# Gate-weight loads of a two-layer kernel issued by GpSimd instead of SyncE

## The chip, the cores and the metric

The program runs on one core of one Trainium2 chip. The metric is the device time of one execution in microseconds (us), median of three runs. The engines are named as the profile names them: PE (TensorE), DVE (VectorE), ACT (ScalarE), POOL (GpSimd) and SP (SyncE, which only issues transfers here). SPq is SP's sequencer.

## The reference, cut to what matters

Two layers on x of shape (8, 256, 128), float32. Each layer is x + s * silu(f), where s is a causal attention and f a mixture of experts, both of the layer-normed x. The change touches the experts of the second layer:

```python
logits = xn @ Wr + br                       # (T, 32)
aff = sigmoid(logits)
top_v, top_i = top_k(aff, 8)
w_full[t, top_i] = top_v / (sum(top_v) + 1e-9)     # gate weight per token and expert
gate = silu(einsum('th,ehi->eti', xn, Wg) + bg)    # 32 experts, 64 inner columns each
up = einsum('th,ehi->eti', xn, Wu) + bu
down = einsum('eti,eih->eth', gate * up, Wd) + bd
routed = einsum('te,eth->th', w_full, down)
```

The kernel multiplies the gate branch of each expert by its token weights before the down projection, so the sum over experts becomes one accumulation on PE.

## The kernel before

The 2048 tokens are cut into 4 chunks of 512. Inner columns stand on the 128 partitions and tokens run along the free axis, so two experts (2 x 64 columns) fill one tile. A chunk has 16 such pairs and a 17th step for the shared expert: step n of `gate`, `up` and `down` is pair n % 17 of chunk n // 17.

The order of all work is one list written out by hand, `PROGRAM` (lines 87 to 141). Every engine walks the same list and does its own part of each step, in that order, waiting on semaphores for the other engines. An engine never goes past a step whose semaphore has not come. The steps that matter here:

- `weights1/c`: PE turns the gate weights of chunk c, ACT copies them, SP stores them in a scratch tensor in HBM (L553).
- `wb/n`: the weights of two pairs are read back from that scratch, each row spread over 64 partitions by a broadcast read. There are two loads, 64 x 2 x 512 float32 each, into slot n % 2 of the two slots of `wb`. The step waits for the store and for `s_ga_done` at 2 (n - 1), which says that the multiplications that read the slot last are done. There are 32 such steps, 64 loads. Before the change they stand on SP at L554 to L563.
- `gate/n`: PE multiplies (L754), ACT makes tanh into `gt` (L1002) and the linear part into `gb` (L1005), POOL multiplies `gb` by the spread weights in `wb` (L1098). It waits for ACT and for both loads of the slot, and counts up `s_ga_done`.
- `up/n`: PE multiplies (L763) after the result of the expert before it is ready, since there is one PSUM bank. DVE makes `h` from `gt` and `gb` (L1274), then from the bank (L1281).
- `down/n`: PE adds `h` times wd to the accumulator (L775).
- `max` and `score`: attention scores in units. DVE takes maxima (L1302), or ACT takes the exponential (L1020) and POOL cuts it to the causal part in place (L1091), in `pk`, which `values` on PE reads (L850).
- `norm/c/b`: POOL raises a 128x32 tile to the power -0.5 (`orms`, L1102); `norm0` and `norm1` do so with a 128x4 tile (L1064, L1075).
- `fetch/c/b`: SP issues 24 loads of split queries and keys into `qa` and `ka` (L540); `store/c` issues the 12 stores before them (L524), `minus/c/b` two small copies (L548).

SP issues everything in this kernel before the change: weights, inputs, stores, fetches and the `wb` loads, all on one queue. POOL issues no transfer. The slots give a `wb` step a place well ahead of its use: `wb/1`, say, comes two list entries after `gate/1`, and the first multiplication that reads it is in `gate/2`. The program reserves 1024 bytes of each partition for descriptors of transfers that POOL issues.

Of the kernel before, what the change touches and what calls it, by code (L numbers as in the profile page):

```python
# [45 lines left out]
E1, INNER = 32, 64  # L46
# [98 lines left out]
def build(nc, t):  # L145

    with ExitStack() as ctx:
# [359 lines left out]
        def _(sp):  # L507
            def steps(program):
                for step in program:
                    kind, c, *rest = step  # L510
                    if kind == "load":
                        if c >= 2:
                            sp.wait_ge(s_var1, at(2 * (c - 2), "var1", 1))
                        sp.dma_start(x_of[side(c)], t["x"][c]).then_inc(s_x_in[c % 2], 16)
                    elif kind == "store":

                        for n in range(2):
                            for a in range(3):
                                done, name = ((s_part1, "part1"), (s_part2, "part2"), (s_part3, "part3"))[a]
                                for f in range(2):  # L520
                                    r = a if n == 0 else 2 - a
                                    sp.wait_ge(done, at(c, name, 2 * n + f + 1))
                                    dst = t["parts_dram"][c, n, f * 2 * GH:(f + 1) * 2 * GH, :, r * DH:(r + 1) * DH, :]
                                    sp.dma_start(dst, parts[:, a, 2 * n + f, :]).then_inc(s_parts_stored[f], 16)  # L524
                    elif kind == "fetch":
                        b = rest[0]
                        for f in range(2):
                            heads = slice(f * 2 * GH, (f + 1) * 2 * GH)
                            sp.wait_ge(s_parts_stored[f], at(c, "parts_stored", 16 * 6))
                            if c:  # L530
                                sp.wait_ge(s_sc_ps, unit(c - 1, b, 2 * f + 1, 2) + 1)
                            else:
                                sp.wait_ge(s_rooms, 3)
                            for n, dst in enumerate((qa, ka)):
                                for m in range(2):
                                    row = m * HALF
                                    for width in (3, 2, 1):
                                        first = 0 if n == 0 else 3 - width
                                        src = t["parts_dram"][c, n, heads, m, first * DH:(first + width) * DH, b * SEQ:(b + 1) * SEQ]
                                        sp.dma_start(dst[row:row + width * DH, b, heads, :],  # L540
                                                     src.rearrange("h r t -> r h t")).then_inc(s_qk_in[b][f], 16)
                                        row += width * DH
                    elif kind == "minus":
                        b = rest[0]
                        sp.wait_ge(s_mrow_sb, at(c, "mrow_sb", b + 1))
                        for m in range(2):
                            row = m * HALF + TERMS
                            sp.dma_start(qa[row:row + 3, b, :, :],  # L548
                                         mrows[m * 3 * HEADS:(m + 1) * 3 * HEADS, b * SEQ:(b + 1) * SEQ]).then_inc(s_mrow_in, 16)
                    elif kind == "weights1":  # L550

                        sp.wait_ge(s_wt_sb, at(c, "wt_sb", 1))
                        sp.dma_start(t["wt_dram"][c], hs[INNER:INNER + E1, c % 2, :]).then_inc(s_wt_stored, 16)  # L553
                    elif kind == "wb":  # L554

                        k, slot = c % (PAIRS // 2), c % 2
                        sp.wait_ge(s_wt_stored, at(c // (PAIRS // 2), "wt_stored", 16))
                        if c >= 2:
                            sp.wait_ge(s_ga_done, 2 * (c - 1))
                        src = t["wt_dram"][c // (PAIRS // 2)].rearrange("(j e) t -> e j t", e=2)  # L560
                        for e in range(2):
                            sp.dma_start(wb[e * INNER:(e + 1) * INNER, slot, :, :],
                                         src[e, 2 * k:2 * k + 2, :].partition_broadcast(INNER)).then_inc(s_wb_in[slot], 16)  # L563
                    elif kind == "fin":
                        sp.wait_ge(s_out_done, at(c, "out_done", 1))
                        sp.dma_start(t["out"][c], out[:, :, :]).then_inc(s_out_stored, 16)
# [473 lines left out]
        def _(pool):  # L1040
# [19 lines left out]
            for step in PROGRAM:  # L1060
# [25 lines left out]
                elif kind == "score":  # L1086
# [3 lines left out]
                    pool.wait_ge(s_pk_done, unit(c, b, g, u) + 1)  # L1090
                    pool.affine_select(out=dst, in_=dst, compare_op=ALU.is_ge, fill=0.0, base=0,  # L1091
                                       pattern=[[0, heads], [1, P]], channel_multiplier=-1).then_inc(s_pk_masked, 1)
                elif kind == "gate" and c % STEPS < PAIRS:
                    j = c % STEPS
                    k = (c // STEPS * PAIRS + j) // 2
# [323 lines left out]
```

## Time and profile before

| what | value |
|---|---|
| median of 3 runs | 533.67 us |
| the runs | 528.33, 536.59, 533.67 us |
| profiled execution, its own time | 529.14 us |
| its span | 527.1 us |
| PE, DVE, ACT, POOL busy | 482.0, 398.0, 286.7, 264.5 us |
| mean granted clock of PE | 0.984 |

The span runs from the first to the last instruction of the profiled execution. Busy time counts an engine's instructions and leaves out waits, branches and the issue of transfers. The three runs lie 1.5% apart. A window is given in microseconds from the start of the span.

### The profile page before, as it was taken

What the parts mean: (1) busy time and instruction counts of PE and PEld (TensorE: products, weight loads), DVE (VectorE), ACT (ScalarE), POOL (GpSimd) and SP (SyncE); (2) the same over time, 40 slices, a digit from 0 to 9 for tenths busy, and PEclk for the clock granted to TensorE, in tenths of its full rate; (3) what the DMA queues carried; (4) which work ended last, traced back from release to release, by engine and by line L of the source; (5) the groups of instructions that cost most, each with busy time, mean ns of one, the idle gap of its engine ahead of it and who ended that gap; (6) DMA issues with size and microseconds to landing.
All of it is one profiled execution on the core that took longest, in us unless ns stands there. A gap on an engine that the chain in (4) does not pass through costs nothing.

```text
span 527.1 us, 8723 instructions
## 1 busy us (share of the span) xinstructions
PE 482.0 (91%) x3104; PEld 234.7 (45%) x3104; DVE 398.0 (76%) x796; ACT 286.7 (54%) x456; POOL 264.5 (50%) x223
## 2 busy tenths in 40 slices
PE   3898798589998999999999999999999999999995
PEld 3645444233543444544344554454344444444442
DVE  2326387788987888677999888569988988977674
ACT  1342563215775644557775654546775556567741
POOL 6040153104634447735767622716754749456962
PEclk9999799889999999999999999999999999999999
DMA  7800149851069553012369083101563561131201
GB/s 281 295 1 0 44 116 156 131 100 45 1 164 141 100 87 81 5 60 62 103 137 158 14 136 65 44 21 42 159 117 90 86 124 42 40 85 40 74 8 41
DMA packets 49627, 46.04 MB, mean 87 GB/s; under 512 B 6352, under 2 KB 39216, under 8 KB 48944
## 3 DMA queue, kind: packets, MB, share of 16 engines
q1 hardware_dynamic: 49584, 45.48, 38.6%
q8 instruction: 25, 0.41, 0.3%
q14 instruction: 18, 0.15, 0.1%
HBM read 37.47 MB, written 7.60 MB: 86 GB/s over the span
## 4 chain that ended last, share of the span: by engine, by line
PE 63%; DVE 16%; issue 6%; POOL 5%; DMA 4%; SPq 3%; ACT 3%; DVEq 0%; POOLq 0%; ACTq 0%
PE bank L763 8%; PE bank L775 8%; PE bank L754 7%; PE scores L795 6%; PE bank L850 4%; PE scores L789 4%; DVE nmax L1302 3%; DVE h L1274 3%; SPq L540 2%; POOL gb L1098 2%; PE scores L690 2%; PE scores L681 2%; PE scores L728 2%; PE scores L684 2%; DMA wb<-wt_scratch 2%
## 5 line engine op out<-in xcount | busy, mean ns | idle before, releaser
L1098 POOL TENSOR_TENSOR gb<-gb,wb 128x512 f32<-128x512 f32 x64 | 83.4, 1303 | 119.7 <-ACT gb L1005 111.4
L1302 DVE TENSOR_REDUCE nmax<-scores 128x4 f32<-128x1024 f32 (+1 forms) x96 | 114.3, 1217 | 20.0 <-PE scores L795 19.6
L1020 ACT ACTIVATE pk<-scores 128x1024 f32<-128x1024 f32 x96 | 95.8, 1023 | 28.2 <-PE scores L795 27.9
L1091 POOL TENSOR_SCALAR_AFFINE_SELECT pk<-pk 128x512 f32<-128x512 f32 (+1 forms) x96 | 82.2, 861 | 45.2 <-ACT pk L1020 44.6
L1002 ACT ACTIVATE gt<-bank,bgh 128x512 f32<-128x512 f32 (+1 forms) x68 | 46.8, 688 | 61.6 <-PE bank L754 49.0
L763 PE MATMUL bank<-xnt,wu 128*128 128x512 f32 x128 | 68.3, 616 | 1.1 <-DVE h L1281 1.1
L754 PE MATMUL bank<-xnt,wg 128*128 128x512 f32 x128 | 68.2, 615 | 0.9 <-ACT gb L1005 0.9
L775 PE MATMUL bank<-h,wd 128*128 128x512 f32 x128 | 68.5, 625 | 0.1
L1274 DVE SCALAR_TENSOR_TENSOR h<-gt,gb 128x512 f32<-128x512 f32 x64 | 56.7, 885 | 10.9 <-POOL gb L1098 10.6
L1281 DVE SCALAR_TENSOR_TENSOR h<-bank,bu,h 128x512 f32<-128x512 f32 x64 | 48.1, 751 | 16.2 <-PE bank L763 14.5
L789 PE MATMUL scores<-mask_h,ident_h 64*128 64x256 bf16 (+2 forms) x384 | 38.4, 279 | 10.1 <-DVE nmax L1302 8.4
L1102 POOL TENSOR_TENSOR orms<-oms,minus_half 128x32 f32<-128x32 f32 x8 | 44.7, 5591 | 0.4 <-DVE oms L1335 0.3
L1005 ACT ACTIVATE gb<-bank,bg 128x512 f32<-128x512 f32 x64 | 43.7, 683 | 0.0
L795 PE MATMUL scores<-ka,qa 48*128 48x256 bf16 (+1 forms) x512 | 38.0, 247 | 0.0
L850 PE MATMUL bank<-pk,v 128*32 128x512 f32 x256 | 34.1, 605 | 1.8 <-DVE o L1322 1.6
L795 PE MATMUL scores<-qa,ka 51*128 51x128 bf16 (+1 forms) x512 | 34.0, 245 | 0.6 <-DVE nmax L1302 0.6
L789 PEld LDWEIGHTS scores<-mask_h,ident_h 64*128 64x128 bf16 x384 | 12.9, 95 | 47.1 <-issue 21.4
L795 PEld LDWEIGHTS scores<-qa,ka 51*128 51x128 bf16 x512 | 16.7, 94 | 36.5 <-issue 16.4
L775 PEld LDWEIGHTS bank<-h,wd 128*128 128x128 f32 x128 | 21.6, 191 | 19.7 <-issue 16.4
L1027 ACT ACTIVATE ot<-bank 128x512 f32<-128x512 f32 x32 | 19.2, 599 | 20.4 <-PE bank L855 20.2
L763 PEld LDWEIGHTS bank<-xnt,wu 128*128 128x128 f32 x128 | 21.2, 189 | 19.7 <-issue 13.4
L1085 POOL TENSOR_TENSOR parts<-qkf,parts 128x512 bf16<-128x512 f32 x16 | 18.9, 1204 | 20.6 <-ACT parts L967 20.6
(247 smaller groups left out, 728.3 us busy)
## 6 DMA issues: line engine op xcount, KB each, us to landing
wb<-wt_scratch SPq DMA_DIRECT2D x64, 256.0 KB, 4.2
parts_scratch<-parts SPq DMA_DIRECT2D x48, 128.0 KB, 2.4
qa<-parts_scratch SPq DMA_DIRECT2D x32, 96.0 KB
ka<-parts_scratch SPq DMA_DIRECT2D x32, 96.0 KB
qa<-parts_scratch SPq DMA_DIRECT2D x32, 64.0 KB
ka<-parts_scratch SPq DMA_DIRECT2D x32, 64.0 KB
ha<-in_wkq SPq DMA_DIRECT2D x1, 1024.0 KB, 4.9
wb<-in_wvo SPq DMA_DIRECT2D x1, 1024.0 KB, 7.4
```

The source lines that it names most:

```text
L754: m = mm(bank[5], wg[:, j * P:(j + 1) * P], xnt1[:, c % 2, :], start=True, stop=True)
L763: mm(bank[6], wu[:, j * P:(j + 1) * P], xnt1[:, c % 2, :], start=True, stop=True).then_inc(s_up_ps, 1)
L775: m = mm(bank[7], wd[:, j, :], h1[:, n % HR, :], start=(j == 0), stop=False)
L789: mm(s[m][:, :, cols - P + part * HALF:cols], ident_h[half, 1 - m + part, :], late.unsqueeze(1).to_broadcast([HALF, per, P - part * HALF]) ...
L795: last = mm(s[m][:, h, :], stat[half, b, h0 + h, row:row + P], move[half, b, h0 + h, tile0:tile0 + width], start=(h == 0 and not masked), ...
L850: mm(o[32 * hh:32 * hh + 32, :, :], v1[:, 2 * b, head, :], pk0[g % 2][:, 2 * hh:2 * hh + 2, :], start=True, stop=False, skip_group_check=True)
L1020: A(dst.rearrange("p (h m) q -> p m h q", m=2), pairs[pair_of(step)][:, :, :].rearrange("p m (h q) -> p m h q", q=cols), ACT.Exp, scale=SC ...
L1091: pool.affine_select(out=dst, in_=dst, compare_op=ALU.is_ge, fill=0.0, base=0, pattern=[[0, heads], [1, P]], channel_multiplier=-1).then_i ...
L1098: pw(gb[:, c % 2, :], gb[:, c % 2, :], wb[:, k % 2, j % 2, :], ALU.mult).then_inc(s_ga_done, 1)
L1274: link(V.scalar_tensor_tensor(out=h, in0=gt[0:rows, n % 2, :], scalar=1.0, in1=gb[0:rows, n % 2, :], op0=ALU.add, op1=ALU.mult))
L1281: V.scalar_tensor_tensor(out=h, in0=up, scalar=bu[0:rows, j:j + 1], in1=h, op0=ALU.add, op1=ALU.mult).then_inc(s_h_done, 1)
L1302: V.tensor_reduce(dst, src, AX, ALU.max, negate=True).then_inc(s_nmax_done, 1)
```

## The change

The branch for `wb` leaves the program of SP and stands in that of POOL, with the same two waits, the same two transfers and the same semaphores. The list is the same, so POOL now issues each pair of loads when it comes to that place among its own multiplications, masks and powers.

```diff
@@ SP @@
-                    elif kind == "wb":
-
-                        k, slot = c % (PAIRS // 2), c % 2
-                        sp.wait_ge(s_wt_stored, at(c // (PAIRS // 2), "wt_stored", 16))
-                        if c >= 2:
-                            sp.wait_ge(s_ga_done, 2 * (c - 1))
-                        src = t["wt_dram"][c // (PAIRS // 2)].rearrange("(j e) t -> e j t", e=2)
-                        for e in range(2):
-                            sp.dma_start(wb[e * INNER:(e + 1) * INNER, slot, :, :],
-                                         src[e, 2 * k:2 * k + 2, :].partition_broadcast(INNER)).then_inc(s_wb_in[slot], 16)
@@ POOL, between the branches for score and gate @@
+                elif kind == "wb":
+
+                    k, slot = c % (PAIRS // 2), c % 2
+                    pool.wait_ge(s_wt_stored, at(c // (PAIRS // 2), "wt_stored", 16))
+                    if c >= 2:
+                        pool.wait_ge(s_ga_done, 2 * (c - 1))
+                    src = t["wt_dram"][c // (PAIRS // 2)].rearrange("(j e) t -> e j t", e=2)
+                    for e in range(2):
+                        nc.gpsimd.dma_start(wb[e * INNER:(e + 1) * INNER, slot, :, :],
+                                     src[e, 2 * k:2 * k + 2, :].partition_broadcast(INNER)).then_inc(s_wb_in[slot], 16)
```

The next rows are the order of instructions on POOL around `wb/0` and `wb/1`, at the first experts of the first chunk. A row has the line, the operation, the tiles and how many stand in a row. Before:

```order
L1064 TENSOR_TENSOR rstd<-vare,minus_half 128x4
L1098 TENSOR_TENSOR gb<-gb,wb 128x512
L1075 TENSOR_TENSOR rstd<-vare,minus_half 128x4
L1098 TENSOR_TENSOR gb<-gb,wb 128x512 x5
L1091 AFFINE_SELECT pk<-pk 128x4x128 x2
```

And with the change, where every line number of POOL is 10 smaller except that of `gate`:

```order
L1091 DMA wb<-wt_scratch 64x2x512 x2
L1054 TENSOR_TENSOR rstd<-vare,minus_half 128x4
L1098 TENSOR_TENSOR gb<-gb,wb 128x512
L1065 TENSOR_TENSOR rstd<-vare,minus_half 128x4
L1098 TENSOR_TENSOR gb<-gb,wb 128x512
L1091 DMA wb<-wt_scratch 64x2x512 x2
L1098 TENSOR_TENSOR gb<-gb,wb 128x512 x2
```

The loads of `wb/0` now come before the power of `norm0/2`, and those of `wb/1` between the multiplications of `gate/1` and `gate/2`.

The second place is POOL late in the last chunk, from `gate/60` to `gate/63`. Before:

```order
L1098 TENSOR_TENSOR gb<-gb,wb 128x512
L1091 AFFINE_SELECT pk<-pk 128x4x128
L1091 AFFINE_SELECT pk<-pk 128x1024
L1102 TENSOR_TENSOR orms<-oms,minus_half 128x32
L1098 TENSOR_TENSOR gb<-gb,wb 128x512
L1091 AFFINE_SELECT pk<-pk 128x4x128 x2
L1098 TENSOR_TENSOR gb<-gb,wb 128x512
L1091 AFFINE_SELECT pk<-pk 128x1024
L1091 AFFINE_SELECT pk<-pk 128x4x128
L1098 TENSOR_TENSOR gb<-gb,wb 128x512
```

With the change:

```order
L1091 DMA wb<-wt_scratch 64x2x512 x2
L1098 TENSOR_TENSOR gb<-gb,wb 128x512
L1081 AFFINE_SELECT pk<-pk 128x4x128
L1081 AFFINE_SELECT pk<-pk 128x1024
L1102 TENSOR_TENSOR orms<-oms,minus_half 128x32
L1091 DMA wb<-wt_scratch 64x2x512 x2
L1098 TENSOR_TENSOR gb<-gb,wb 128x512
L1081 AFFINE_SELECT pk<-pk 128x4x128 x2
L1098 TENSOR_TENSOR gb<-gb,wb 128x512
L1091 DMA wb<-wt_scratch 64x2x512 x2
L1081 AFFINE_SELECT pk<-pk 128x1024
L1081 AFFINE_SELECT pk<-pk 128x4x128
```

The loads of `wb/29`, `wb/30` and `wb/31` stand ahead of `gate/60`, ahead of `gate/61` and behind `gate/62`.

## Rows read from the trace of the kernel before

**Rows 1.** The page: busy time of each engine, then the chain that ended last.

```profile
PE 482.0 (91%) x3104; PEld 234.7 (45%) x3104; DVE 398.0 (76%) x796; ACT 286.7 (54%) x456; POOL 264.5 (50%) x223
...
PE 63%; DVE 16%; issue 6%; POOL 5%; DMA 4%; SPq 3%; ACT 3%; DVEq 0%; POOLq 0%; ACTq 0%
```

**Rows 2.** Stretches: window, length, busy PE, PEld, DVE, ACT, POOL, clock, DMA, GB/s.

```profile
77.00:105.00 28.00, 20.05 (x118) 10.61 (x118) 20.07 (x48) 9.82 (x19) 9.24 (x8) 0.92 0.87 140
...
485.00:502.00 17.00, 16.60 (x99) 6.98 (x98) 11.47 (x18) 13.53 (x19) 17.00 (x13) 1.00 0.26 63
```

**Rows 3.** Waits: who waited for whom, total us, times, longest us.

```profile
SPq L559 <- POOL gb L1098: 130.5, 16, 20.3
...
PE scores L789 <- DMA ka<-parts_scratch: 1.4, 1, 1.4
```

**Rows 4.** The tile wb: duration ns min/median/max, first and last start; landing.

```profile
L562 SPq DMA_DIRECT2D wb<-wt_scratch x64: 573/607/643, 77.0 to 498.5; - x64
L1098 POOL TENSOR_TENSOR gb<-gb,wb x64: 1257/1270/1774, 82.3 to 510.2; 128x512 f32<-128x512 f32 x64
...
DMA to landing us min/median/max: 3.6/4.2/9.6
```

**Rows 5.** Timeline of POOL, 76 to 101: start, us, what, [idle before <- releaser].

```profile
76.74 2.50 POOL L1081 TENSOR_TENSOR pk<-pk 128x512 f32<-128x512 f32 x2 [2.22 <-ACT pk L937]
...
82.26 1.26 POOL L1098 TENSOR_TENSOR gb<-gb,wb 128x512 f32<-128x512 f32 x1 [1.60 <-DMA wb<-wt_scratch]
...
90.87 1.26 POOL L1098 TENSOR_TENSOR gb<-gb,wb 128x512 f32<-128x512 f32 x1
98.51 2.48 POOL L1098 TENSOR_TENSOR gb<-gb,wb 128x512 f32<-128x512 f32 x2 [6.37 <-DMA wb<-wt_scratch]
```

**Rows 6.** Timeline of DVE and PE, 99 to 104.

```profile
99.87 1.66 DVE L1274 SCALAR_TENSOR_TENSOR h<-gt,gb 128x512 f32<-128x512 f32 x1 [3.08 <-POOL gb L1098]
...
103.51 0.50 PE L789 MATMUL scores<-mask_h,ident_h 64*128 64x256 bf16 x4 [5.33 <-DVE nmax L1302]
```

**Rows 7.** Timeline of POOL, 436 to 448.

```profile
436.48 1.68 POOL L1091 TENSOR_SCALAR_AFFINE_SELECT pk<-pk 128x1024 f32<-128x1024 f32 x2
...
439.72 5.83 POOL L1102 TENSOR_TENSOR orms<-oms,minus_half 128x32 f32<-128x32 f32 x1 [0.29 <-DVE oms L1335]
...
446.56 1.27 POOL L1098 TENSOR_TENSOR gb<-gb,wb 128x512 f32<-128x512 f32 x1
```

**Rows 8.** Timeline of DVE and PE behind that, at experts 51 and 52.

```profile
450.60 0.75 DVE L1281 SCALAR_TENSOR_TENSOR h<-bank,bu,h 128x512 f32<-128x512 f32 x1 [0.54 <-PE bank L763]
...
452.25 1.02 PE L763 MATMUL bank<-xnt,wu 128*128 128x512 f32 x2
```

**Rows 9.** Timeline of POOL, DVE and PE around `wb/27` and `gate/57`.

```profile
468.21 1.09 POOL L1091 TENSOR_SCALAR_AFFINE_SELECT pk<-pk 128x1024 f32<-128x1024 f32 x1 [0.85 <-ACT pk L1020]
...
474.28 0.68 DVE L1274 SCALAR_TENSOR_TENSOR h<-gt,gb 128x512 f32<-128x512 f32 x1
...
479.30 1.12 PE L763 MATMUL bank<-xnt,wu 128*128 128x512 f32 x2
```

**Rows 10.** Timeline of POOL and DVE, 480 to 502.

```profile
480.99 2.19 POOL L1091 TENSOR_SCALAR_AFFINE_SELECT pk<-pk 128x1024 f32<-128x1024 f32 x2
484.92 1.27 POOL L1098 TENSOR_TENSOR gb<-gb,wb 128x512 f32<-128x512 f32 x1 [1.73 <-ACT gb L1005]
484.94 1.80 DVE L1274 SCALAR_TENSOR_TENSOR h<-gt,gb 128x512 f32<-128x512 f32 x1
...
493.63 1.27 POOL L1098 TENSOR_TENSOR gb<-gb,wb 128x512 f32<-128x512 f32 x1
...
501.21 1.04 DVE L1274 SCALAR_TENSOR_TENSOR h<-gt,gb 128x512 f32<-128x512 f32 x1 [0.43 <-POOL gb L1098]
```

**Rows 11.** DVE's L1274: the page's group, then its durations ns min/median/max.

```profile
L1274 DVE SCALAR_TENSOR_TENSOR h<-gt,gb 128x512 f32<-128x512 f32 x64 | 56.7, 885 | 10.9 <-POOL gb L1098 10.6
...
L1274 DVE SCALAR_TENSOR_TENSOR h<-gt,gb x64: 673/683/1797, 83.6 to 513.0; 128x512 f32<-128x512 f32 x64
```

## The prediction

> **What bounds the kernel now.** I read the page first. PE is busy 91% of the span and POOL half of it, and the chain that ended last runs 63% on PE, 16% on DVE and 5% on POOL [rows 1]. POOL has 262 us of idle time, so its added work costs only where another engine waits for it. The windows show where that may be. Near the start, from 77 to 105, PE is busy 20.05 of 28 us and the DMA engines 0.87 of the time. From 485 to 502 POOL is busy 17.00 of 17 us [rows 2]. Then the waits: SP stands 130.5 us before `wb` steps, waiting for POOL's multiplications to free a slot, while PE waits only 1.4 us for any transfer [rows 3]. So the time that SP gets back buys little. Last, the tile `wb`: SP takes 0.607 us to issue one load, POOL 1.27 us for one multiplication, and a load lands 4.2 us after its issue (3.6 to 9.6) [rows 4].
>
> **The change, part by part.** SP loses 64 issues of 0.607 us, 39 us, and its 130.5 us of waits [rows 3, 4]. Queued behind them on SP are the `fetch`, `store` and `minus` steps. They may come earlier, but PE waits 1.4 us in all for such a load [rows 3]. I count nothing for it and keep the 1.4 us for a rival.
>
> POOL gains 64 issues, two at each of 32 places. No row shows a transfer issued by POOL. The low bound is SP's 0.607 us, the high one 4.2 us, if POOL were held until the load has landed [rows 4]. I take 1.3 us, from the nearest row of POOL's own, the 1.27 us multiplication [rows 4]. A pair then costs 2.6 us and all of them 83 us, which would bring POOL to 348 us busy, 66%. The Trainium skill, page "DMA: Bandwidth & Descriptors", section "Latency and other measured facts", gives about 1 us to the first byte of a transfer issued by POOL and 0.6 us for one by SP; SP's row agrees, and an estimate of the sum with 1.0 us an issue is 8 us in place of the 12 below.
>
> The added wait for `s_ga_done` costs nothing by itself: at each place in the list POOL has already run the multiplications that it counts, as the places below show. What is new is that a load starts when POOL gets there, and that everything of POOL behind it starts later. The data is there 1.3 + 4.2 = 5.5 us after the place (the second load's issue starts 1.3 us in). Three places are priced.
>
> Start. POOL reaches `wb/0` at 76.74 + 2.50 = 79.24, so the data lands at 84.7 and `gate/0` starts 2.5 us later than its 82.26 [rows 5]. DVE waits for it, and what follows shifts. `gate/1` then ends at 92.13 + 2.5 = 94.6, which is the place of `wb/1`; its data comes at 100.1 with the median landing, 1.6 us after the 98.51 at which `gate/2` starts now, and at 105.5, 7.0 us after, with the longest landing of 9.6 us, which is that of this very load in a full queue [rows 4, 5]. DVE waits 3.08 us for this `gate/2` and PE 5.33 us for DVE [rows 6], so the lateness reaches PE. The two ends are 1.6 and 7.0; nothing places it nearer to one, since its own queue is new and the DMA engines are as full as before. I take the middle, 4.3 us.
>
> `wb/24` and `wb/25`. They stand between the two masks that start at 436.48 and ahead of the power at 439.72. One more mask stands there, at half of 1.68 us. So the power cannot start before 436.48 + 1.68 + 0.84 + 5.2 = 444.2, 4.5 us late. POOL then runs to `gate/51` without idle time, so that starts at 451.1 instead of 446.56 and ends at 452.3 [rows 7]. DVE's two operations of 0.68 and 0.75 us then end at 453.8, against 451.35 [rows 8, 11]; PE's next `up`, at 452.25, had 0.9 us to spare [rows 8]. On the path: 2.4 - 0.9 = 1.5 us.
>
> `wb/29` to `wb/31`. `wb/29` comes at 480.99 + 2.19 = 483.18, POOL is free at 485.8, and `gate/60` moves from 484.92 by 0.9 us. From there POOL has no idle time. `wb/30` stands before `gate/61` at 493.63 and `wb/31` before `gate/63`, 2.6 us each, and DVE waits for `gate/63` at 501.21 [rows 2, 10]. Nothing is left to take the lateness up: 0.9 + 2.6 + 2.6 = 6.1 us.
>
> Elsewhere it is hidden. `wb/27` is the closest case: place 469.30, data 474.8, `gate/57` done at 476.1, 1.8 us after DVE took it, and DVE's second operation ends near 477.6, before PE's next `up` at 479.30 [rows 9]. If that cover of 1.7 us were gone, the rest of 1.8 us would go on the path, as it would at two or three places like it.
>
> Sum: 4.3 + 1.5 + 6.1 = 11.9 us. The profiled execution took 529.14 us for a span of 527.1, so the changed one would take 541.0. It lies 4.5 us under the median of 533.67, and the changed kernel's runs will scatter in the same way, so I forecast 533.67 + 11.9 = **546 us** for the median. With 0.607 us an issue the same places give about 1 + 0 + 2.4 us, 537; with 2.6 us, twice my value, about 6 + 8 + 14 us, 562.
>
> **The rivals.** About 2%, 10.7 us, is what a measurement of this kernel can tell from no change; the bounds are 523.0 and 544.3.
>
> My forecast's mechanism with its own range, 538 to 551: 0.40. It straddles the bound, with half on each side.
>
> *Absorbed.* POOL is idle half of the time and an issue costs hardly more than on SP: 537. For it speaks that most `wb` places have 5 us or more to the first use; against it, that 485 to 502 has no idle time. 0.25. The Trainium skill says, on the same page, section "Issuing engines are not separate DMA queues", that a change of the issuing engine saves or costs only the sequencer's time, usually a small one; this would be that case.
>
> *DVE is held too.* One L1274 takes 1.80 us beside a POOL multiplication at 484.94 where its median is 0.683 [rows 10, 11]. All 64 take 56.7 us against 64 x 0.683 = 43.7, 13 us more, beside 264.5 us of POOL work. If an issue holds DVE as a multiplication does, 83 us of them add 13 x 83 / 264.5 = 4 us there, and as much in DVE's other operations: 546 + 8 = 554, if it all lies on the path; 0.12. The Trainium skill, page "SBUF — State Buffer", section "SBUF: two separate sides", has DVE and POOL share a port pair that one locks for a whole instruction, and warns that some DVE copies keep POOL from writing descriptors. The trace agrees for POOL's computing; no row shows an issue.
>
> *A dear issue.* At 2.6 us each, 562; 0.12. If POOL is held until each load has landed, 4.2 us, it has 269 us more work than now and would be the bound in order: the last three pairs alone cost 24 us, the whole over 590; 0.04.
>
> *Faster.* The loads get a queue of their own. Before, `wb/1` took 9.6 us behind the 24 fetch loads of SP and POOL stood idle 6.37 us for it [rows 4, 5]. If POOL's loads are served in turn with SP's and an issue is as cheap as on SP, `gate/2` comes earlier, at most by the 3.08 us that DVE waits; with PE's 1.4 us for `ka` that is 4.5 us [rows 3, 6], 529 us. It decides the sign only where an issue costs less than about 0.6 us, so that the late stretch costs nothing. The Trainium skill, page "DMA: Bandwidth & Descriptors", section "Queues, rings and completion order", says that a DMA engine takes its queues in turn, which speaks for it; no row has two queues at work. 0.07, of which 0.03 is over 2% faster.
>
> That the change does not do what it says is excluded: the order of POOL has all 64 loads.
>
> **How the numbers follow.** Faster by over 2%: 0.03. Slower by over 2%: half of the forecast's 0.40 and a little of its upper side, 0.22, and the three dear cases, 0.12 + 0.12 + 0.04, together 0.50. Within 2%: the rest, 0.47. The range, 8 times in 10, reaches from the cheap end, 533, to the twice as dear issue, 562; left out are most of the faster case, the longest case and half of the dear one.
>
> **What would show it.** Rows of POOL issuing `wb` near 1.3 us confirm the price; at 0.6 or 2.6 the sum fails there. The start term is right if `gate/2` starts 2 to 7 us later than 98.51; the late one if POOL has no idle time between `gate/60` and `gate/63` and that stretch is 5 to 7 us longer, with DVE's wait for L1098 above its 10.6 us. DVE is held too if L1274's mean rises above 885 ns. The forecast is wrong if POOL's sequencer waits long before the loads, if the loads land later than 4.2 us, or if PE's idle time does not grow while POOL's does.

## The result: 570.5 us, outside the range

The changed kernel took 570.49 us (median of 4 runs, 568.73 to 577.32) beside 533.77 us for the kernel before on the same chip: ratio 1.0695, 95% interval [1.0596, 1.0794]. Run again it took 569.8 us, ratio 1.0716 [1.0644, 1.0789]. The forecast was 546 us with a range of 533 to 562. The direction was right, and the size was wrong by a factor of three: 37 us in place of 12. The profile after is that of the repeated run, because the profiled execution of the first was a disturbed one. Its span is 568.6 us, 41.5 more than before; the traces show more than the 37 us of the medians, since the profiled execution of the kernel before lay 4.5 us under its median.

The page of the changed kernel, busy time and then the chain that ended last, the answer to [rows 1]:

```profile
PE 498.7 (88%) x3104; PEld 241.0 (42%) x3104; DVE 407.8 (72%) x796; ACT 287.3 (51%) x456; POOL 299.8 (53%) x287
...
PE 52%; POOL 13%; DVE 12%; issue 9%; DMA 8%; ACT 4%; SPq 1%; POOLq 0%; DVEq 0%; ACTq 0%
```

POOL is busy 35 us longer, but that is not the loss by itself: POOL is still idle for almost half of the span. PE has the same 3104 instructions and is busy 16.7 us longer, at a mean granted clock of 0.950 where it was 0.984. The other 24.8 us are idle time of PE.

Its tile `wb`, the answer to [rows 4]: duration ns min/median/max, first and last start, then the landing.

```profile
L1091 POOL DMA_DIRECT2D wb<-wt_scratch x64: 587/596/805, 82.0 to 537.9; - x64
L1098 POOL TENSOR_TENSOR gb<-gb,wb x64: 1250/1268/1776, 91.1 to 551.7; 128x512 f32<-128x512 f32 x64
...
DMA to landing us min/median/max: 3.5/4.2/9.6
```

An issue costs POOL 0.596 us, less than half of the 1.3 us that I took and no more than it cost SP. The median landing is as before. So neither number of the sum was worse than assumed, and the loss was still three times the sum.

Its waits, the answer to [rows 3]: who waited for whom, total us, times, longest us.

```profile
POOL gb L1098 <- DMA wb<-wt_scratch: 28.1, 5, 9.1
DVE h L1274 <- POOL gb L1098: 26.9, 8, 6.9
...
POOL wb L1091 <- DMA wb<-wt_scratch: 6.4, 2, 3.6
```

POOL waited 8.0 us for its loads before and 28.1 now, and DVE's wait for POOL went from 10.6 [rows 11] to 26.9.

The start, the answer to [rows 2, 5]: first two windows (us, busy time of PE, PEld, DVE, ACT, POOL, clock, DMA share, GB/s), then the timeline of POOL.

```profile
77.00:105.00 28.00, 19.54 (x81) 10.24 (x79) 14.99 (x44) 9.64 (x19) 10.00 (x11) 0.82 0.87 144
105.00:160.00 55.00, 45.04 (x316) 22.02 (x316) 42.09 (x72) 19.89 (x32) 19.66 (x22) 0.81 0.28 69
```

```profile
81.96 1.40 POOL L1091 DMA_DIRECT2D wb<-wt_scratch  x2
...
91.12 1.26 POOL L1098 TENSOR_TENSOR gb<-gb,wb 128x512 f32<-128x512 f32 x1 [6.71 <-DMA wb<-wt_scratch]
...
100.94 1.25 POOL L1091 DMA_DIRECT2D wb<-wt_scratch  x2
111.33 2.48 POOL L1098 TENSOR_TENSOR gb<-gb,wb 128x512 f32<-128x512 f32 x2 [9.15 <-DMA wb<-wt_scratch]
```

`wb/0` is in place 9.0 us after its first issue and `gate/0` starts 8.9 us later than before. `gate/2` starts at 111.33, 12.8 us later where I had 2 to 7. By `gate/4` it is 15.9 us. PE runs 81 and 316 matmuls in these two windows, where it ran 118 [rows 2] and 402, and its granted clock is 0.82 and 0.81, against 0.92 [rows 2] and 0.95.

The late stretch, the answer to [rows 7, 10], timeline of POOL around `gate/51`, and around `gate/60` to `gate/63`:

```profile
473.59 5.46 POOL L1102 TENSOR_TENSOR orms<-oms,minus_half 128x32 f32<-128x32 f32 x1
...
480.08 2.48 POOL L1098 TENSOR_TENSOR gb<-gb,wb 128x512 f32<-128x512 f32 x2
...
523.03 1.28 POOL L1098 TENSOR_TENSOR gb<-gb,wb 128x512 f32<-128x512 f32 x1
...
531.31 1.25 POOL L1091 DMA_DIRECT2D wb<-wt_scratch  x2
...
540.13 1.26 POOL L1098 TENSOR_TENSOR gb<-gb,wb 128x512 f32<-128x512 f32 x1
```

`gate/60` starts 38.1 us later than before and `gate/63` 40.7, so this stretch adds 2.6 us where I had 5.2.

Last, a thing that the trace of before does not have. DVE, POOL and PE around 280 in the changed kernel:

```profile
278.43 1.25 POOL L1091 DMA_DIRECT2D wb<-wt_scratch  x2
279.69 2.28 POOL L1075 TENSOR_TENSOR parts<-qkf,parts 128x512 bf16<-128x512 f32 x2
281.92 1.27 POOL L1098 TENSOR_TENSOR gb<-gb,wb 128x512 f32<-128x512 f32 x1
283.14 0.63 POOL L1081 TENSOR_SCALAR_AFFINE_SELECT pk<-pk 128x512 f32<-128x512 f32 x1
...
280.31 3.49 DVE L1320 TENSOR_TENSOR rl<-rl,lam 128x8 f32<-128x8 f32 x1
...
284.31 1.07 PE L840 MATMUL bank<-pk,v 128*32 128x512 f32 x8 [2.62 <-DVE o L1322]
```

A DVE instruction on 8 columns, 0.17 us elsewhere, takes 3.49 us. It starts in the first of the four POOL instructions behind the issues and ends at 283.80, when the last of them ends at 283.77 and POOL stands idle; until then POOL has no gap. PE then waits 2.62 us. The changed kernel has 8 DVE instructions of this kind between 2.0 and 3.5 us long. Before, the longest of the kind is the 1.80 us of [rows 10].

Where the 41.5 us arise, read from the start of each multiplication against before: 15.9 up to `gate/4`, 16.6 from there to `gate/49`, 1.8 to `gate/56`, 3.8 to `gate/60`, 2.6 to `gate/63`, 0.8 behind it.

### The profile page after: what moved, and what is told of

It is laid out like the page before. It is cut to its first block, busy times and chain, and to the rows that moved or that the text cites. A ratio compares the mean times of both kernels' runs of the same rounds, so it can differ in the third digit from the quotient of the medians.

```text
span 575.6 us, 8723 instructions
## 1 busy us (share of the span) xinstructions
PE 501.5 (87%) x3104; PEld 242.1 (42%) x3104; DVE 409.4 (71%) x796; ACT 287.7 (50%) x456; POOL 299.9 (52%) x287
## 4 chain that ended last, share of the span: by engine, by line
PE 51%; POOL 13%; DVE 12%; DMA 9%; issue 9%; ACT 4%; SPq 2%; POOLq 0%; DVEq 0%; ACTq 0%
PE bank L744 6%; DMA wb<-wt_scratch 6%; PE bank L753 5%; PE bank L765 5%; PE scores L785 5%; POOL pk L1081 4%; POOL gb L1098 4%; PE scores L779 3%; PE bank L840 3%; DVE nmax L1302 3%; PE scores L671 3%; PE scores L674 3%; PE scores L718 2%; POOL orms L1102 2%; PE scores L680 2%
## 5 line engine op out<-in xcount | busy, mean ns | idle before, releaser
L1098 POOL TENSOR_TENSOR gb<-gb,wb 128x512 f32<-128x512 f32 x64 | 82.2, 1287 | 125.9 <-ACT gb L995 97.3
L1081 POOL TENSOR_SCALAR_AFFINE_SELECT pk<-pk 128x512 f32<-128x512 f32 (+1 forms) x96 | 81.0, 851 | 41.8 <-ACT pk L1010 41.3
L1274 DVE SCALAR_TENSOR_TENSOR h<-gt,gb 128x512 f32<-128x512 f32 x64 | 58.5, 913 | 28.3 <-POOL gb L1098 28.2
L753 PE MATMUL bank<-xnt,wu 128*128 128x512 f32 x128 | 69.5, 625 | 3.7 <-DVE h L1281 3.6
L744 PE MATMUL bank<-xnt,wg 128*128 128x512 f32 x128 | 70.3, 632 | 0.9 <-ACT gb L995 0.9
L765 PE MATMUL bank<-h,wd 128*128 128x512 f32 x128 | 69.8, 635 | 0.1
L779 PE MATMUL scores<-mask_h,ident_h 64*128 64x256 bf16 (+2 forms) x384 | 40.5, 292 | 11.0 <-DVE nmax L1302 8.8
L1091 POOL DMA_DIRECT2D wb<-wt_scratch x64 | 39.3, 616 | 7.6 <-DMA wb<-wt_scratch 6.5
L785 PE MATMUL scores<-ka,qa 48*128 48x256 bf16 (+1 forms) x512 | 40.2, 259 | 0.0
L785 PEld LDWEIGHTS scores<-qa,ka 51*128 51x128 bf16 x512 | 16.7, 94 | 42.8 <-issue 21.4
```

Of the source, the lines that this page charges most:

```text
L744: m = mm(bank[5], wg[:, j * P:(j + 1) * P], xnt1[:, c % 2, :], start=True, stop=True)
L753: mm(bank[6], wu[:, j * P:(j + 1) * P], xnt1[:, c % 2, :], start=True, stop=True).then_inc(s_up_ps, 1)
L765: m = mm(bank[7], wd[:, j, :], h1[:, n % HR, :], start=(j == 0), stop=False)
L779: mm(s[m][:, :, cols - P + part * HALF:cols], ident_h[half, 1 - m + part, :], late.unsqueeze(1).to_broadcast([HALF, per, P - part * HALF]) ...
L785: last = mm(s[m][:, h, :], stat[half, b, h0 + h, row:row + P], move[half, b, h0 + h, tile0:tile0 + width], start=(h == 0 and not masked), ...
L1098: pw(gb[:, c % 2, :], gb[:, c % 2, :], wb[:, k % 2, j % 2, :], ALU.mult).then_inc(s_ga_done, 1)
```

## The experiments

Each ratio is against the kernel before on the same chip (medians 531.3 to 532.8 us).

**The changed kernel again**, without an edit.

> The changed kernel again, for a trace beside the following ones. All theories: 566 to 574 us, ratio 1.06 to 1.08, POOL's issue of a load near 0.6 us.

569.8 us, told above.

**A larger ring for descriptors.**

```diff
-    nc = _bacc.Bacc(..., dynamic_dma_scratch_size=1024)
+    nc = _bacc.Bacc(..., dynamic_dma_scratch_size=2048)
```

> The changed kernel with 2048 bytes of each partition for the descriptors of POOL's transfers in place of 1024. In the trace of the changed kernel POOL waited before an issue until an earlier load had landed, twice, 6.5 us in all (at wb/3 and wb/15). Theory ring: POOL stands there because at most three loads fit; with twice the room both waits vanish and the time falls by 1 to 4 us, to 566 to 569. Theory place: the room does not matter, time unchanged within 1 us of the changed kernel.

566.9 us, 1.0625 [1.0554, 1.0695]. In the changed kernel POOL waited twice, 3.6 us at most and 6.4 in all, ahead of a load while three others were in flight; with 2048 bytes it does not. That is 3 us of the 37 by the medians; the two intervals overlap.

**The first two steps on SP.** `wb/0` and `wb/1` are issued by SP at their old places, the other 60 loads by POOL.

```diff
+                    elif kind == "wb" and c < 2:        # SP
+                        ... the two loads, then_inc(s_wb_sp[c], 16)
-                elif kind == "wb":                      # POOL
+                elif kind == "wb" and c >= 2:
```

> The changed kernel with wb/0 and wb/1 (4 of the 64 loads) issued by SP at their old places, the other 60 by POOL. In the changed trace gate/8 already stood 16 us later than before, of which my prediction had 4.3. Theory start: these four loads land late (9 and 10 us beside the fetches on the other queue) and the idle PE loses its clock, so the time falls by 12 to 17 us, to 553 to 558, and the granted clock from 77 to 160 us returns from 0.81 to above 0.92. Theory spread: the cost is in POOL's issues all along, so 4 of 64 loads give back 5 us at most, 565 or more.

561.45 us, 1.0547 [1.0483, 1.0611]: the start is worth 8 us, and 29 us lie elsewhere. That is between the ranges of both theories. The granted clock from 77 to 105 came back to 0.98, that from 105 to 160 only to 0.85.

**Early places.** POOL walks a list in which each `wb/n` but 0, 1, 2, 3 and 16 stands right behind the multiplication that frees its slot.

```diff
+            rest.insert(rest.index(("gate", j // PAIRS * STEPS + j % PAIRS)) + 1, ("wb", n))
-            for step in PROGRAM:
+            for step in POOL_PROGRAM:
```

> The changed kernel with POOL walking a list of its own in which wb/n, for all n but 0, 1, 2, 3 and 16, stands right behind the multiplication that frees its slot, where SP issued it at the earliest. POOL still issues 64 loads. Theory place: from gate/8 to the end the changed kernel loses some 30 us because loads start late and land after they are wanted; with early places no multiplication waits for a load after wb/3, and 12 to 25 us come back, 545 to 558. Theory issue: what costs is POOL's time for 64 issues and DVE held beside it, so the time stays above 563.

564.99 us, 1.0592 [1.0526, 1.0658]. The waits of gates 27, 57 and 59 for their loads, 3.8 to 4.5 us each, are gone, and only 5 us come back. Late places were not the main cause, as far as this kernel shows, which still has the long holds described above.

**Late, but on SP**, and **issues on POOL, but nothing late**, and **both**. In the first, SP issues the real loads and also waits for the last POOL instruction that stands ahead of the place. In the second, SP issues the real loads as before, and POOL issues two loads of 32 bytes a row into a tile that nobody reads at each place (64 more small transfers).

```diff
+                        kind, m, *rest = pool_before(c)
+                        if kind == "gate":
+                            sp.wait_ge(s_ga_done, gates(m) + 1)
+                        ... likewise for masks, powers and the others
```

```diff
+                    for e in range(2):
+                        nc.gpsimd.dma_start(toy[e * INNER:(e + 1) * INNER, slot, :, :],
+                                     src[e, 2 * k:2 * k + 2, 0:8].partition_broadcast(INNER)).then_inc(s_toy[slot], 16)
```

> The kernel before, SP issues all loads, but each wb step on SP also waits until POOL has done the last instruction that stands ahead of that step in its list: the loads start when POOL comes to the place, and POOL issues nothing. Steps of SP behind a wb step are held with it. Theory place: lateness alone makes the slowdown; 550 to 565 us. Theory both: lateness is about half of what is left beside the start, 540 to 550. Theory issue: lateness is hidden, within 4 us of the kernel before.

> The kernel before, with 64 further loads issued by POOL at the 32 wb places, as many pieces each, but 32 bytes a piece (0.26 MB in all instead of 16.8) into a small tile that nothing reads. SP still issues the real loads at its old places. POOL is as busy as in the changed kernel, nothing comes late. Theory issue: POOL's 39 us fill its gaps, POOL runs without a break more often, DVE operations with both inputs in SBUF are held by it, PE goes idle and loses its clock: 545 to 556 us, L1274's mean above 900 ns. Theory place: within 4 us of the kernel before.

> Both edits of the two kernels beside it: SP's loads wait for POOL's place and POOL issues 64 small loads. What is still missing against the changed kernel is the second queue beside the fetches. Theory both, added up: the sum of the two slowdowns within 5 us, about 558 to 566; if one mechanism does it all, no more than the larger of the two.

Late alone: 552.25 us, 1.0383 [1.0335, 1.0431]. Small issues alone: 557.97, 1.0491 [1.0432, 1.055]. Both: 580.9, 1.0896 [1.0827, 1.0966], 48.6 us more than before where the two alone add up to 45.7. The last two are above their expected ranges, 545 to 556 and 558 to 566: my theories priced the issues too low. The first has a confound that I saw only in its trace: SP's other steps queue behind the late ones (SP stands 96.6 us for masks and 47.0 for multiplications at these places), which the changed kernel does not have. Its trace has no DVE instruction over 1.9 us. The second is the finding: 39 us of small issues on an engine that is idle half of the time, with nothing late, cost 26 us.

**Early, with the first two on SP.** Both edits together.

> The changed kernel with wb/0 and wb/1 on SP and early places on POOL for the others (but 2, 3, 16), 60 loads issued by POOL. Each edit alone gave back 8 and 5 us. If start and lateness are separate, both come back: 555 to 558 us, and the 23 us that stay belong to POOL's issues. If the early places gave back only time at the start by chance, 561 or more.

555.95 us, 1.0444 [1.0389, 1.0498]. With lateness gone at both ends, 24 us stay.

**Memsets in the place of the issues.** The kernel before, and at each `wb` place the same waits and two memsets of 128x640 bf16 on POOL (632 ns each, 40.4 us in all, 1 us more than the issues).

```diff
+                    for e in range(2):
+                        if c + e > 0:
+                            pool.wait_ge(s_toy, 2 * c + e)
+                        pool.memset(toy[:, :], 0.0).then_inc(s_toy, 1)
```

> The kernel before (533) with the waits of the 32 wb steps and two memsets of 128x640 bf16 behind each on POOL, some 0.65 us each by the 418 ns for 384 elements, so POOL is as much longer occupied (about 40 us) as by the 64 small loads, which cost 26 us, but nothing is transferred and no descriptor written; SP issues the real loads as before. If POOL's time at those places is what costs, with DVE held behind POOL's unbroken runs: 555 to 562. If the small loads cost by what a load does beyond the time of POOL (its descriptors, its packets among the other queues', a wait for the ring): 533 to 542.

535.72 us, 1.0071 [1.0032, 1.0111]. My own first theory, that POOL's time at those places costs, falls: the same time without transfers costs 4 us, not 26. The two traces can be laid side by side at one place, behind the power of `norm1/2`. With the small issues (DVE, then POOL):

```profile
252.10 5.02 DVE L1163 TENSOR_SCALAR tmp<-x,mv,rstd 128x128 f32<-128x128 f32 x4 [0.22 <-POOL rstd L1077]
257.04 0.68 DVE L1287 SCALAR_TENSOR_TENSOR h<-gt,gb 128x512 f32<-128x512 f32 x1
...
251.97 1.25 POOL L1104 DMA_DIRECT2D toy<-wt_scratch  x2
253.22 2.33 POOL L1093 TENSOR_SCALAR_AFFINE_SELECT pk<-pk 128x512 f32<-128x512 f32 x3
255.53 1.25 POOL L1111 TENSOR_TENSOR gb<-gb,wb 128x512 f32<-128x512 f32 x1
```

With memsets:

```profile
251.26 1.33 DVE L1161 TENSOR_SCALAR tmp<-x,mv,rstd 128x128 f32<-128x128 f32 x4 [0.19 <-POOL rstd L1077]
252.52 1.11 DVE L1285 SCALAR_TENSOR_TENSOR h<-gt,gb 128x512 f32<-128x512 f32 x1
...
251.11 1.34 POOL L1103 MEMSET toy<- 128x640 bf16 x2
252.41 2.75 POOL L1093 TENSOR_SCALAR_AFFINE_SELECT pk<-pk 128x512 f32<-128x512 f32 x3
```

With memsets DVE asks at 252.52 while a mask runs, gets in between this mask and the next (1.11 us, of which 0.43 is the wait), and the masks take 2.75 us in place of 2.33, since now POOL waits. In the kernel with small issues, one of the four `tmp` instructions starts at about 253.35, in the first mask, and does not end before 256.8, when the three masks and the multiplication are through. One of the four takes 3.52 us.

I then counted, in the traces of the kernel before and of the eighteen experiments, the DVE instructions that took over 0.1 us more than their shortest and had begun in a POOL instruction with another less than 60 ns behind it, and asked whether DVE got in between the two. The rows part the cases by whether POOL had issued a transfer and not paused for 50 ns since:

```
                                              DVE got in   DVE was held on
no issue in POOL's unbroken run (19 traces)       453             0
an issue in the run                                23            93
```

Those held on waited through two (42), three (38), four (12) or five (1) POOL instructions, the one in which they began included; in the last case, and in three others, that is the issue itself, in its last 80 ns. In 66 cases POOL then paused, in 27 DVE got in without that. The largest pause since the issue among the 93 is 27 ns. In 149 of the 453 cases POOL had issued before and then paused by itself, for 189 ns at least and with nothing written in between, so a pause alone is enough at that length.

Sixteen cases without an issue are not in the first row. In fourteen of them DVE began in the last 60 ns of a POOL instruction, less than 30 ns before the record of the next one begins, and waited through that one. In the other two, in the kernel with memsets, DVE ended just behind the first memset and took 0.91 and 1.15 us, where 0.17 and 0.34 are the shortest. The kernel before and the kernel with memsets have no DVE instruction of this kind over 1.9 us; the one with small issues has 7, up to 3.74 us.

**One small issue a place, the last eight steps only, and the best placing with the larger ring.**

```diff
-                    for e in range(2):
+                    for e in range(1):       # e10: one small issue, 32 in all
```

```diff
+                elif kind == "wb" and c >= 24:      # e11: POOL; SP issues wb/0 to wb/23
```

> The kernel before with one small load at each wb step on POOL instead of two (32 in all, about 20 us of POOL). If the loss goes with POOL's added time: half of the 26 us, 544 to 548. If it is a threshold, that is if the first issue of a place falls into POOL's slack and only the second closes the gap that DVE gets in by: below 540.

> Loads wb/24 to wb/31 are issued by POOL as in the change, wb/0 to wb/23 by SP as before: the two late terms of the prediction alone. By the prediction's working at the measured 0.6 us an issue, some 2.4 us: 533 to 537. If POOL's added time costs everywhere alike, by its share of 8 in 32 of the 29 us that the kernel with only wb/0 and wb/1 on SP lost: 539 to 542. If most of the loss lies before the last quarter, as the slips of the small issues have it (23 of 26 us before gate/36): 534 to 537 as well, so above 538 speaks against both.

> The best placing with POOL as issuer (wb/0 and wb/1 on SP, the others right behind the multiplication that frees their slot; 556) with the ring of 2048 bytes. If the ring still holds issues where places lie close together, it gives the 3 us that it gave the changed kernel: 552 to 554. If no fourth load is in flight at those places: 555 to 557. In no case under 540, since the 39 us of issues stay on POOL.

One small issue: 545.14 us (runs from 540.9 to 549.7), ratio 1.0199 [1.0104, 1.0294], with 4 of the long holds. It fits half of the loss and tells little more. The last eight steps: 542.65 us, 1.0217 [1.0138, 1.0296], above the 537 that two of the three theories allowed, and just above the 542 of the third. Nothing differs from before up to 436 except 2 us. Then come two long holds (3.30 and 3.32 us) and late loads at gates 57 and 59. Here the hold of 3.30 us, DVE first, then POOL, some 6 us behind the last issue:

```profile
449.55 3.30 DVE L1356 TENSOR_TENSOR on<-oc,orms 128x512 f32<-128x512 f32 x1
...
443.31 5.46 POOL L1116 TENSOR_TENSOR orms<-oms,minus_half 128x32 f32<-128x32 f32 x1
448.75 1.09 POOL L1092 TENSOR_SCALAR_AFFINE_SELECT pk<-pk 128x1024 f32<-128x1024 f32 x1
449.81 2.48 POOL L1112 TENSOR_TENSOR gb<-gb,wb 128x512 f32<-128x512 f32 x2
```

The issues end at 443.30 and the power starts at 443.31. The last of these loads landed at 447.06, before the hold begins. So neither the issue nor its transfer is still going on: the time since is long, but POOL has not paused. The larger ring with early places: 560.47 us, 1.054 [1.0458, 1.0622], no better than with the small one, a miss.

**A break behind the issues.** POOL writes a tile of 8 columns and waits for its own write. In the kernel with small issues (e13), in the changed kernel (e14), and in that with early places, the first two steps on SP and the larger ring (e15).

```diff
+                    pool.memset(brk[:, :], 0.0).then_inc(s_brk, 1)     # behind the two dma_start
+                    pool.wait_ge(s_brk, c + 1)
```

> The 64 small loads beside the real ones on SP (558), and behind each pair POOL writes a tile of 8 columns and waits for its own write, a break of some 50 to 70 ns in its run. If an issue holds DVE until POOL's run has a break, and a break so short is enough: no DVE instruction over 1.9 us where there were 8, and 537 to 543, which is the 536 of the memsets and a little for the 32 writes. If the break must be longer (27 ns were too short, 432 enough), or if the holds are not what costs: 556 to 562, with the holds at the same places.

> The changed kernel (570) with the same break behind each pair. If the break frees DVE: the 20 us or so that the holds cost come back, 548 to 554, and what is left is the late landing, at the start above all. Otherwise 568 to 574.

> wb/0 and wb/1 on SP, the other places early, ring of 2048 bytes (560), with the same break. If the break frees DVE: 537 to 543, since nothing lands late here and POOL's time is worth the 4 us of the memsets. Otherwise 557 to 563.

536.74 us, 1.0068 [1.0036, 1.0099], where it was 557.97. 551.6 us, 1.034 [1.0275, 1.0405], where it was 569.8. 540.55 us, 1.0135 [1.0098, 1.0173], where it was 560.5. All three came as the theory said (537 to 543, 548 to 554, 537 to 543; the first 0.3 us under it), and none of the three traces has a hold over 1.9 us. The same place with small issues and the break, DVE and then POOL:

```profile
253.37 1.17 DVE L1167 TENSOR_SCALAR tmp<-x,mv,rstd 128x128 f32<-128x128 f32 x4 [0.22 <-POOL rstd L1079]
254.42 0.68 DVE L1291 SCALAR_TENSOR_TENSOR h<-gt,gb 128x512 f32<-128x512 f32 x1
...
253.23 1.25 POOL L1106 DMA_DIRECT2D toy<-wt_scratch  x2
254.47 0.12 POOL L1108 MEMSET brk<- 128x8 f32 x1
254.67 2.56 POOL L1095 TENSOR_SCALAR_AFFINE_SELECT pk<-pk 128x512 f32<-128x512 f32 x3
```

The break is 75 to 86 ns without work. The 18 us that it gives back to the changed kernel are net of the 0.2 us of POOL's time that it takes at each of 32 places.

**The break ahead of the issues, the break alone, and the start on SP with the break.**

```diff
+                    pool.memset(brk[:, :], 0.0).then_inc(s_brk, 1)     # e16: ahead of the two dma_start
+                    pool.wait_ge(s_brk, c + 1)                         # e17: no dma_start on POOL at all
```

> The kernel of e13 (537) with the same break ahead of each pair of small issues instead of behind it, so the same instructions in another order. If an issue makes the run behind it closed to DVE until a break: the holds of over 1.9 us are back and the time with them, 554 to 562. If breaks in POOL's work help DVE wherever they stand: 535 to 541.

> The kernel before (533) with the 32 breaks at the places of wb on POOL and no issue there. If the break only undoes what an issue does: 532 to 536. If breaks let DVE in more often also where nothing is issued and that is worth something: 526 to 531.

> The changed kernel with the break (552) and wb/0 and wb/1 issued by SP as before. The start was worth 8 us without the break; with its slip of 10.8 us at gate/4 down to some 2: 541 to 545, of which 4 are POOL's time and the rest the late landings at gates 27, 57 and 59. If the start's delay is taken up elsewhere: 548 to 552.

Ahead of the issues: 558.71 us, 1.0533 [1.0482, 1.0584], with 6 long holds. In the other order the same instructions give nothing back. The place of above, DVE and then POOL, where three masks and the multiplication hold `h`, which takes 4.13 us:

```profile
254.78 4.13 DVE L1291 SCALAR_TENSOR_TENSOR h<-gt,gb 128x512 f32<-128x512 f32 x1
...
253.22 0.09 POOL L1104 MEMSET brk<- 128x8 f32 x1
253.61 1.25 POOL L1108 DMA_DIRECT2D toy<-wt_scratch  x2 [0.29 <-POOL brk L1104]
254.87 2.26 POOL L1095 TENSOR_SCALAR_AFFINE_SELECT pk<-pk 128x512 f32<-128x512 f32 x3
257.10 1.26 POOL L1115 TENSOR_TENSOR gb<-gb,wb 128x512 f32<-128x512 f32 x1
```

The break alone: 530.47 us, 0.9966 [0.9935, 0.9998], the one version that is not behind the kernel before, by 0.3% and at the edge of its interval. That lies in the range of the second theory (526 to 531), by which breaks help a little where nothing is issued too; it is 2 us, against 18 and 21 us behind issues. So the break mainly undoes what an issue does. The start on SP with the break: 541.65 us, 1.0189 [1.0143, 1.0235], 10 us under the changed kernel with the break.

## Why the prediction was wrong

The 37 us, as the runs take them apart: 18.2 by the break (569.8 to 551.6), 10.0 by the start on SP (551.6 to 541.65), and 9 left, of which some 4 are POOL's plain time (4.4 with the memsets, 4.0 with the small issues and the break).

The 18.2 are not all long holds. Against the changed kernel, the trace with the break stands 5.1 us better at `gate/4`, where neither trace has had a long hold yet (the first of the changed kernel, 1.90 us, is at 153.6): `gate/2` got its load 2.4 us earlier, and the granted clock from 105 to 160 was 0.91 in place of 0.81. What brings this is not shown. From `gate/4` to `gate/49`, where most of the holds are, it gains 12.5 us, and behind that 0.8.

The remaining 5 fit the late loads of gates 27, 57 and 59 only in part. The kernel of e15 has early places, the larger ring, the start on SP and the break, so no such load is late in it. Its profiled execution is 5.0 us shorter than that of the kernel with the start on SP and the break, of which 5.3 arise from `gate/56` to `gate/60`; by the medians it is only 1.1 us shorter (540.55 and 541.65). So the late loads are worth between 1 and 5 us.

- **The price of an issue** was twice too high, 1.3 us against 0.596. The range's cheap end had it right. My "SP's row agrees" compared two different things: the row of 0.607 us is the time of an issue, not the time to a first byte. With the true price my working would have given 537, further from the truth. The price was not what decided.
- **"Elsewhere it is hidden"** is the step that failed. From `gate/4` to `gate/49` I counted nothing and 16.6 us arose, of which the break takes away 12.5. I had looked at each place for the data's landing and for POOL's own lateness, and both are mostly covered there. What I did not ask is what the issues do to the POOL instructions behind them. A hold of 3.5 us in a DVE instruction that gates `up` or `values` exceeds any cover of 1 or 2 us.
- **DVE is held too** was a rival at 0.12 and 554 us. The mechanism has the right two engines and the wrong form. I scaled it by POOL's busy time, as if an issue held DVE while it lasts. L1274's mean went from 885 ns [rows 11] to 913 and DVE's busy time by 9.8 us, close to the 8 us of the rival. But its few long holds fall in the path. The rule on the page "SBUF — State Buffer", section "SBUF: two separate sides", of the Trainium skill has the port pair locked for one instruction; the trace agrees as long as nothing is issued (all 453 cases of the table), and differs behind an issue, where up to four instructions in a row held DVE.
- **The start** was mis-sized: 4.3 us in the sum, 10.0 by the runs. I moved `wb/0` by 2.5 us with the median landing of 4.2, and it took 9.0 us beside SP's loads; before, its data came 5.1 us after its first issue, and it was `wb/1` that took 9.6 [rows 4]. Both steps now take 9 us or more. *Faster* fell with it: a queue of its own brought POOL's loads no earlier.
- **PE's clock** was not in the sum. It fell to 0.82 and 0.81 in the windows behind the start, and at its lower level (a granted clock of 0.50 from 395 to 397 in the kernel with early places) the eight multiplications of `values` of 1.06 us take 1.93. PE's busy time grew by 16.7 us with the same instructions, two fifths of the 41.5. This is no further term beside those above: part of it comes back with them (PE is busy 491.7 us with the break, 489.9 with the start on SP too).
- **`wb/24`, `wb/25`**: 0.7 us arose between `gate/49` and `gate/52`, where I had 1.5. **`wb/29` to `wb/31`**: 2.6 us from `gate/60` to `gate/63`, where I had 5.2 with twice the price. Both are near what the working gives with 0.6 us an issue. **`wb/27`**, named as the closest case and costed at nothing: `gate/57` slips by 3.6 us, of which 1.1 are left at `gate/58`; `gate/59` then slips by 3.3 for `wb/28`, and 3.8 are left of both at `gate/60`.
- **Absorbed**, 0.25, did not hold: the issues' plain time is worth 4 us of 37. The Trainium skill, page "DMA: Bandwidth & Descriptors", section "Issuing engines are not separate DMA queues", says that issuing from several engines only saves the sequencers' time to issue; here moving the issues to POOL saved SP 39 us of them and cost the kernel 37.
- **SP's gain**: no run shows any, as I had it.

What stays open is what in the chip makes the difference. The runs show that an issue changes it, that a small write with a pause of 75 to 86 ns behind it changes it back, that a pause of 189 ns or more does so alone, and that one of 27 ns does not. Between 27 and 189 ns no run parts the pause from the write. In 23 of 116 cases DVE got in all the same, and in 27 of the 93 it got in later without a pause; what tells these apart I can't say. Why the first loads land so late is open as well. One trace bears on it: with the late places on SP the loads of `wb/0` (issued at 81.67) and `wb/1` (96.88) were all in place 5.1 and 5.3 us after the first issue, with SP's fetches ahead of them or behind them in the same queue; from POOL it was 9.0 and 10.3 us beside those fetches.

## What to carry to other kernels

An issue moved to GpSimd is to be priced by what follows it there: if GpSimd goes on without a pause, a VectorE instruction can wait through several of its instructions instead of one. So let GpSimd write a few columns and wait for that write behind the issue, or keep the issue on SyncE, which was the faster of the two here (533 us against 540.6 at best). An engine that is idle half of the time says nothing of that, and an edit costed at nothing at 25 of 32 places needs a look at who shares a port with the moved instruction. To tell an instruction's time from its side effects, put another of the same length in its place.

## What the runs showed of the hardware

- Behind a transfer issued by POOL, DVE mostly does not get in between the next two POOL instructions: 93 held and 23 not, against 0 and 453 without an issue since POOL's last pause. The longest such instruction took 4.13 us; one of 3.30 us began when its loads had landed.
- A pause of 75 to 86 ns, a small write that POOL waits for, ends this at every place (none held of the 32 to 37 cases in each of the four kernels that have it behind each pair).
- Memsets of bf16 on POOL did not hold DVE in the place shown: four instructions ran beside two memsets in 1.33 us, as they took 1.65 in the kernel before. Two others ended only behind a memset (0.91 and 1.15 us).
- POOL issues a broadcast load to 64 partitions in 0.596 us, SP in 0.607.
- With 1024 bytes for descriptors the fourth load in flight waited; with 2048 it did not, worth 3 us by the medians of the changed kernel (its intervals overlap) and nothing with early places.
- Beside SP's fetches POOL's first two pairs were in place 9.0 and 10.3 us after the first issue, as SP's own `wb/1` was after 10.2; SP's `wb/0` took 5.1.
